# Sorting the targets of a sparse graph attention in two groups by node, with the edge marks made by ScalarE

## What is computed

```python
hs = layer_norm(x, ln1_scale, ln1_bias)          # sources
ht = layer_norm(h_target, ln1_scale, ln1_bias)   # targets
q = (ht @ Wq + bq) / sqrt(32); k = hs @ Wk + bk; v = hs @ Wv + bv
logits = where(adj != 0, q.k per head, -1e30)
ctx = softmax(logits) @ v
ht = layer_norm(ht + ctx @ Wo + bo, ln2_scale, ln2_bias)
out = layernorm(x + ht + gelu(ht @ W1) @ W2)
```

## Time and profile before

| | |
|---|---|
| median of 3 runs | 369.51 us (369.49 to 371.01) |
| profiled execution, its own time | 366.63 us |
| its span in the trace, first to last instruction | 364.8 us |
| busy: PE, DVE, ACT, POOL | 68%, 64%, 43%, 52% |
| first gather | 132.75 us |
| start of the last gather | 289.67 us |

### The profile page before, as it was taken

How to read it: one execution, slowest core, us unless ns; L and a number is a source line. 1 busy time by engine, 2 the same in 40 slices (tenths; PEclk the granted TensorE clock), 3 DMA queues, 4 the chain that set the end, 5 groups by cost and what they waited for, 6 DMA issues and landing times. The chain is left out here.

```text
span 364.8 us, 4184 instructions
## 1 busy us (share of the span) xinstructions
PE 247.2 (68%) x1270; PEld 180.3 (49%) x1270; DVE 233.4 (64%) x648; ACT 157.8 (43%) x263; POOL 191.1 (52%) x209
## 2 busy tenths in 40 slices
PE   0339959897995020325999895879987979679900
PEld 0314413433431010215888785768876967578800
DVE  2613078989489854697798677767878679922110
ACT  0816403698766930002566652646534445223200
POOL 2699704325120037777778878887888712311210
PEclk9999967999999555555999998998999899969965
DMA  7993398999993017776765555555654610000000
GB/s 182 380 386 138 136 320 324 351 417 331 401 353 115 1 51 233 227 204 195 208 199 155 173 139 168 155 158 175 200 153 131 163 34 16 15 0 16 26 24 1
DMA packets 27972, 64.34 MB, mean 176 GB/s; under 512 B 6500, under 2 KB 14950, under 8 KB 25895
## 3 DMA queue, kind: packets, MB, share of 16 engines
q0 software_dynamic: 8368, 29.11, 27.5%
q1 hardware_dynamic: 11792, 25.44, 18.9%
q10 hardware_dynamic: 7782, 9.45, 7.3%
HBM read 53.50 MB, written 12.58 MB: 181 GB/s over the span
## 5 line engine op out<-in xcount | busy, mean ns | idle before, releaser
L610 POOL DMA_INDIRECT arena<-kv_scratch,places x79 | 92.8, 1175 | 22.7 <-issue 22.7
L797 PE MATMUL score<-h_t,w_sb 128*128 128x128 f32 x512 | 70.8, 298 | 7.3 <-ACT h_t L1073 7.2
L797 PEld LDWEIGHTS score<-h_t,w_sb 128*128 128x128 f32 x512 | 66.6, 211 | 10.6 <-ACT h_t L1073 10.6
L709 PE MATMUL bank<-arena 128*128 128x512 f32 x128 | 64.5, 643 | 10.8 <-POOLq L553 5.6
L806 PE MATMUL bank<-w_sb,gelu_t 128*128 128x256 f32 x256 | 58.3, 381 | 0.0
L806 PEld LDWEIGHTS bank<-w_sb,gelu_t 128*128 128x128 f32 x256 | 47.6, 190 | 7.9 <-ACT gelu_t L1049 1.9
L709 PEld LDWEIGHTS bank<-arena 128*128 128x128 f32 x128 | 25.6, 205 | 40.2 <-issue 39.0
L1359 DVE TENSOR_TENSOR arena<-arena,tab 128x1024 f32<-128x1024 f32 (+3 forms) x22 | 24.5, 1113 | 16.9 <-DMA arena<-kv_scratch,places 16.9
L627 POOL DMA_INDIRECT out_dram<-y_out,places x16 | 18.5, 1154 | 28.7 <-ACT y_out L1065 25.9
L606 POOL DMA_INDIRECT tab<-tab_scratch,places x16 | 15.6, 974 | 33.4 <-DVE place_value L1335 28.9
L991 ACT ACTIVATE gelu_t<-arena 128x2048 bf16<-128x2048 bf16 x16 | 30.6, 1910 | 3.8 <-issue 2.3
(11 more groups left out here) (127 smaller groups left out, 378.7 us busy)
## 6 DMA issues: line engine op xcount, KB each, us to landing
arena<-in_adj_dram SPq DMA_DIRECT2D x16, 1024.0 KB, 11.5
kv_scratch<-arena ACTq DMA_DIRECT2D x16, 256.0 KB, 5.5
tab_scratch<-arena ACTq DMA_DIRECT2D x16, 256.0 KB, 4.8
arena<-in_x_dram SPq DMA_DIRECT2D x4, 512.0 KB, 6.6
arena<-in_L_gnn_h_target_dram SPq DMA_DIRECT2D x4, 512.0 KB, 8.8
tab_scratch<-in_x_dram SPq DMA_DIRECT2D x1, 2048.0 KB, 13.8
w_sb<-in_L_gnn_W_dram SPq DMA_DIRECT2D x2, 1024.0 KB, 14.7
arena<-kv_scratch,places POOLq DMA_INDIRECT x79, 3.9
```

The costliest lines, as they stand in the source:

```text
L610: pool.indirect_dma_start(kv_ring[:, ring_at[m] + j, :], None, kv_dram[:, :], at).then_inc(gathered[m][piece], 16)
L709: mm = pe.matmul(proj_ps[n % 2], h_t[:, s, c % 2, k, i * P:(i + 1) * P], weights[:, k, :], start=(k == 0 and s == 0), stop=(k == DK - 1))
L797: mm = pe.matmul(hid_ps[2 * (n % 2) + half][:, f % 4 * P:(f % 4 + 1) * P], w1_sb[:, k, f * P:(f + 1) * P], h2_t[:, n % 2, k, :], start=(k ...
```

## The change

Targets are split by node. **Group A** holds nodes 0 to 1023 (adjacency tiles 0 to 7), of which the 128 with most sources are put off; it has 7 tiles with 2, 3, 3, 4, 5, 5, 7 slots (29). **Group B** holds the rest and those 128, in 9 tiles with 2, 3, 3, 4, 5, 5, 7, 8, 16 slots (53). Slots grow from 79 to 82, gathers from 95 to 98. Group A is sorted before the first gather; group B's quarters, its sort and its matmuls are written into steps -3 to 3 of the second stage (`PLACED` = 3). POOL waits for group A's places before step -3 and for group B's in step 3, behind that step's `rsqrt_pair`.

`find_edges` becomes one ACT pass, Relu(1 - 1e7 x), with its sum as an accumulated output, in place of DVE's pass and ACT's count. Adjacency loads 4 to 15 move from SP's queue to ACT's, each written behind a `find_edges`; from tile 10 on only two slots are left. SP takes over the saves of key and value rows, and the first four adjacency loads wait for the weights. Projection units are reordered (`UNITS`: source chunks ahead of target chunks); the last target unit is projected around group A's placement matmul.

```diff
-    SLOTS = [16, 8, 7, 6, 5, 5, 5, 4, 4, 4, 3, 3, 3, 2, 2, 2]
+    SLOTS_OF = [[7, 5, 5, 4, 3, 3, 2], [16, 8, 7, 5, 5, 4, 3, 3, 2]]
+    SKIPPED = [1, 0]
...
+    UNITS = [(0, 0), (1, 0), (0, 1), (0, 2), (1, 1), (0, 3), (1, 2), (1, 3)]
+    FIRST_UNITS = 6
...
+            def group_ready(g):
+
+                pool.wait_ge(places_ready, 3 * (g + 1))
+                pool.wait_ge(x_copied[g], 16)
+                for r in range(CT):
+                    pool.wait_ge(qh_saved[r], 16 * 2 * (g + 1))
+                if g == 0:
+                    pool.wait_ge(kv_read, TILES)
+                    for r in range(CT):
+                        pool.wait_ge(kv_saved[r], 16 * CHUNKS)
+                    pool.wait_ge(mean_saved, 16)
...
                         rsqrt_pair(pair_of_res(s + 1) if s + 1 < hi else pair_of_y(s - 1), some)
                     if lo == 0:
+                        if step == PLACED:
+                            group_ready(1)
...
+            for u in range(FIRST_UNITS):
+                project(u)
+                if u == 2:
+                    make_keys(0)
+                if u == 4:
+                    make_keys(1)
+                turn_rows(u + 2)
+            project(FIRST_UNITS)
...
+            sum_classes(0)
+            sum_ranks(0)
+            project(FIRST_UNITS + 1, range(2))
+            place(0)
+            project(FIRST_UNITS + 1, range(2, CT))
+            make_keys(2)
...
+                    if lo == 0:
+                        if s == PLACED - 5:
+                            make_keys(3)
+                        if s == PLACED - 3:
+                            sum_classes(1)
+                        if s == PLACED - 1:
+                            place(1)
...
+            def load_adj(t):
+                if t < TILES:
+                    act.wait_ge(edges_ready, (t - AR if t < EARLY + 2 else t - 2) + 1)
+                    act.dma_start(adj_tile_of(t), adj[t * P:(t + 1) * P, :]).then_inc(adj_loaded[adj_slot(t)], 16)
+
+            def find_edges(t):
+
+                act.wait_ge(adj_loaded[adj_slot(t)], 16 * adj_uses(t))
+                edges_free(act, t)
...
+                act.activation(edges_of(t), adj_tile_of(t), ACT.Relu, bias=1.0, scale=-STEEP,
+                               accum_out=tally[:, 0, t:t + 1]).then_inc(edges_ready, 1)
+                if t >= EARLY + 1:
+                    load_adj(t + 1)
...
+                    if lo == 0 and s < -1:
+                        find_edges(TILES - 4 if s == -LEAD else TILES - 2)
+                        find_edges(TILES - 3 if s == -LEAD else TILES - 1)
...
+                        if s == PLACED - 4:
+                            for n in range(QK):
+                                pick_bank(3, n)
+                            split_keys(3)
+                        if s == PLACED - 3:
+                            list_edges(3)
+                            sort_classes(1)
+                        if s == PLACED - 2:
+                            spread_totals(1)
+                        if s == PLACED - 1:
+                            sort_ranks(1)
+                        if s == PLACED:
+                            keep_places(1)
```

More of the change, by code:

```diff
@@ L47, in graph_attention @@
     COLS = sum(2 + s for s in SLOTS)
-    col_of = [sum(2 + s for s in SLOTS[:i]) for i in range(TILES)]
+    col_of = [sum(2 + s for s in SLOTS[:i]) for i in range(TILES + 1)]
+    COLS_OF = [col_of[FIRST_TILE[g + 1]] - col_of[FIRST_TILE[g]] for g in range(2)]
     QUARTERS = 4
@@ new lines, in sum_ranks, with place @@
+            def sum_ranks(g):
+                rows = NCLS * CELLS_OF[g]
+                pe.wait_ge(class_spread, g + 1)
+                pe.matmul(rank_ps[g][:, 0:rows], class_total[0:rows, :], below[0:rows, 0:rows], start=False, stop=True,
+                          skip_group_check=True).then_inc(rank_summed, 1)
+            def place(g):
+                pe.wait_ge(spread_ready, sum(len(set(SLOTS_OF[o])) for o in range(g + 1)))
+                for c in range(CELLS_OF[g]):
+                    if c % QT == 0:
+                        pe.wait_ge(lo_ready, g * CELLS_OF[0] // QT + c // QT + 1)
+                    mm = pe.matmul(place_ps[g][:, 0:COLS_OF[g]], lo_hot[:, c, :], spread[:, c, 0:COLS_OF[g]], start=(c == 0),
+                                   stop=(c == CELLS_OF[g] - 1))
+                mm.then_inc(placed, 1)
@@ L1235, in _ @@
+            for u in range(3):
+                row_stats(u)
+                row_moments(u)
             dve.wait_ge(weights_loaded, 16 * N_WEIGHTS)
@@ L1323, in _ @@
-            dve.wait_ge(pick_step, listed + 10)
-            for d in sorted(set(SLOTS), reverse=True):
-                spread_class(SLOTS.index(d), SLOTS.count(d))
-            for g in range(CELLS // QT):
-                some = slice(QT * g, QT * (g + 1))
-                dve.tensor_tensor(lo_hot[:, some, :],
-                                  rank_lo[:, some].rearrange("p (c a) -> p c a", a=1).to_broadcast([P, QT, P]),
-                                  numbers[:, :].rearrange("p (a n) -> p a n", a=1).to_broadcast([P, QT, P]),
-                                  ALU.is_equal).then_inc(lo_ready, 1)
```

782 lines of the change are left out of this document (451 added, 331 removed).

## The result

| | before | after |
|---|---|---|
| median | 369.99 us (369.49 to 371.01, 4 runs) | 407.45 us (403.52 to 409.75, 4 runs) |
| profiled execution, its own time | 366.63 us | 409.51 us |
| its span | 364.8 us | 407.8 us |
| first gather | 132.75 us | 115.78 us |
| root of step 3 | 207.22 us | 217.43 us |

The ratio is 1.097, 95% interval 1.087 to 1.108: slower by a tenth. The forecast was 390 us, with a range of 366 to 403.

A forecast was written before the change was run, and what follows sets the result against it. The prediction took POOL's gathers to set the pace from 133 to 291 us, at 1.46 us a row. It summed 104 + 100.4 + 181.2 to a 385.6 us span, plus 4.7 to about 390 us, range 366 to 403.

The forecast's parts named there:

- Sign and mechanism: Whole kernel: first gather 29 us earlier, 26 lost until step 3, 24 more for 17 more rows left; slower 0.81.
- From the first gather to the root of step 3: Second stage's start, with group B's quarters and sort between steps on DVE: 100.4 us, against 74.5 before.
- The value of 7 us: Time taken for each 1 MB adjacency load ahead of ACT's last passes, three of them one after another.
- The estimate of 6.8 us: Same 1 MB load, with half of the DMA rate left beside the gathers; the sum would be unchanged.
- The 4.4 us for 1 MB alone: Same load by a fixed 2.0 us plus bytes/436e3; the sum would be 8 us less.
- Until the first gather: First stage, by PE's units, ACT's passes and group A's sort: 104 us (97 to 113), against 132.75 before.
- the first stage does not come forward: Rival, first stage: ACT bounds it or its issues block; first gather 115 to 120; with slow loads, chance 0.15.
- From the root of step 3 to the end: Rest of the second stage and tail: 181.2 us against 157.6, from 17 more rows, one more save, 2.6 less tail.
- the edge that the prediction named as a sign of being wrong: POOL's gathers of group B: the prediction is wrong if rows come at less than 1.4 us each.
- The forecast said that DVE keeps up: Behind step 3's root: DVE needs 8 us of edges and 2.6 of statistics a step, against POOL's 13 us.
- The correction from span to median: Added to the span: 1.8 us to the execution's own time and 2.9 more to the median, 4.7 in all.
- The rival of POOL's pace: Rival, second stage: group B fits DVE's idle time, step 3's root 74.5 us after first gather; 364 us, chance 0.14.

The follow-up runs named there:

- one_pass: Kernel before, with DVE's compare and ACT's count replaced by one ACT pass for the edge marks, nothing else of the change: 372.43 us, 0.8% slower.
- again: The changed kernel once more, unedited, to measure its own spread: 404.01 us, ratio 1.095 to the kernel before.
- h_first: Changed kernel, with the last h_target quarter's load ahead of three late weight loads and the third key/value save on SP's queue: 398.93 us, ratio 1.078.
- place_first: Changed kernel, with PE's `place(0)` ahead of both halves of the last projection instead of between them: 405.93 us, ratio 1.101.
- busy: Kernel before, with 80 repeats of a small DVE operation added right behind the places: 385.42 us, ratio 1.037.
- roots_first: Changed kernel, h_target load and late passes forward, group B sorted in one piece, ten tab slots, each step's rows behind its root: 366.73 us, ratio 0.997.
- load_ahead: Changed kernel, adjacency loads from tile 10 issued ahead of the previous tile's pass but behind the wait for that tile: 405.70 us, ratio 1.098.
- load_first: Changed kernel, adjacency loads from tile 10 issued ahead of ACT's wait for the tile before, passes where they were: 399.92 us, ratio 1.081.
- passes_early: Changed kernel, adjacency loads from tile 10 ahead of the wait for the tile before, passes 12 to 15 moved earlier: 394.56 us, ratio 1.067.

## Why the prediction was half right

**Sign and mechanism: right.** The split was forecast to win at the first gather and to lose more behind it, POOL having nothing to gather while DVE sorts group B between steps.

**From the first gather to the root of step 3: right, term by term.** Forecast 100.4 us, measured 101.65. Pass 12 was put at 16.3 us behind the first gather and began at 17.7; three loads at 7 us each measured 7.1, 7.1 and 7.3; the root of step -1 was put at 52.3 and began at 52.8. The other marks, forecast in brackets: root of step 0 at 64.1 (64.5), of step 1 at 71.7 (73.6), of step 2 at 87.1 (88.5), the places at 95.6 (93). One term did not fit the others: POOL was to wait ahead of the root of step -1 from 35 to 48 us, although that root was put at 52.3; it waited from 31.7 to 52.8, and its rows of group A ended at 75 us, not at 60. Neither moved the sum, since DVE set it.

The value of 7 us carried this stretch, and it was a choice between the least, 5.0, and the median, 11.5, of the earlier trace rows, which no row settled: with either of these the sum would have been 94 or 114 us. That it hit was in part luck. The estimate of 6.8 us from the Trainium skill's page "DMA: Bandwidth & Descriptors", section "Queues, rings and completion order", was nearly as near. Its reason, that the gathers take half of the rate, is not borne out: the third load took 7.3 us from 147.65 us on, and POOL's last gather before it had been issued at 146.47 us. The 4.4 us for 1 MB alone come from that page's section "Anatomy of one DMA", which states the formula for DMAs issued by GpSimd, while these loads are ACT's and SP's; the shortest adjacency load of any run took 4.7 us (one_pass).

**Until the first gather: the step that failed.** Forecast 104 (97 to 113), measured 115.78, 11.8 us of the 22.2 us by which the span came out longer. The sum took the order of units on PE and ACT's passes into account, but put SP's queue at nothing: the last h_target chunk stands there behind `save_kv(2)`. That wait on SP is worth 7.9 us against the profiled execution and 9.7 against again (h_first); without it the first gather is at 107.85, within the forecast's bounds, and the time at 398.93, within the range. The other 3.9 us were not taken apart. The mean row, which the prediction called hidden behind the sort, was so only because the half projection in front of `place(0)` was longer: with that away it was the last (place_first). The rival "the first stage does not come forward" gave 115 to 120 us and 402 to 406 us; the first gather came out there and the time 1.5 us above, but its mechanism, ACT's issues and passes as the bound, is not what the runs showed.

**From the root of step 3 to the end: mis-sized.** Forecast 181.2, measured 190.4. Of these 9.2 us, 4.7 lie before the last gather. The groups of POOL there, by form, first of before, then of after:

```profile
L610 POOL DMA_INDIRECT arena<-kv_scratch,places x41 | 50.2, 1224 | 11.5 <-issue 11.5
L627 POOL DMA_INDIRECT out_dram<-y_out,places x7 | 8.6, 1231 | 2.1 <-issue 2.1
L620 POOL TENSOR_TENSOR rstd_late<-var_late,minus_half 128x2 f32<-128x2 f32 x8 | 5.9, 733 | 0.2
L606 POOL DMA_INDIRECT tab<-tab_scratch,places x4 | 3.8, 955 | 1.2 <-issue 1.2
```

```profile
L710 POOL DMA_INDIRECT arena<-kv_scratch,places x53 | 58.0, 1095 | 15.3 <-issue 15.0 <-DVE var_late L1676 0.3
L706 POOL DMA_INDIRECT tab<-tab_scratch,places x9 | 10.9, 1216 | 2.5 <-issue 2.5
L727 POOL DMA_INDIRECT out_dram<-y_out,places x8 | 9.6, 1200 | 3.8 <-ACT y_out L1248 1.9 <-issue 1.5 <-DVE var_late L1676 0.3
L720 POOL TENSOR_TENSOR rstd_late<-var_late,minus_half 128x2 f32<-128x2 f32 x9 | 9.6, 1066 | 14.1 <-DVE var_late L1676 14.0
```

A row cost (58.0 + 15.3 + 10.9 + 2.5)/62 = 1.40 us, less than the 1.46 forecast and at the edge that the prediction named as a sign of being wrong, so that the rows added 20.0 us for 24.8. Three other terms ran over. The sum had left out that one more root comes with one more save, and the roots are 1066 ns each for 733: 3.7 us for nothing. The saves added 2.7 us for 1.45. And POOL waits for DVE: of the 14.0 us, 9.55 stand ahead of step 3's root, the other 4.5 are new. The forecast said that DVE keeps up.

The other 4.5 us are the tail, 77.0 for 72.5. One step was gone from it, as forecast (five roots behind the last gather for six), but this saved nothing: the last context came 31.4 us behind the last gather for 31.2, and the end 45.7 us behind that for 44.0. At the statistics of one step DVE now waits 2.74 us for PE (355.05 us), for 0.34 before (313.77 us).

**The correction from span to median** (4.7 us) did not hold: after, the median lay 0.35 us below the profiled span. This was luck: the miss of the span was 22.2 us, that of the time 17.5.

**The rival of POOL's pace** needed group B to fit into DVE's idle time. It did not in any order that was run. The extra 26.6 us of DVE's work come at a time when POOL's root, and with it POOL, waits for DVE, and of 26.4 us added there to the kernel before, 14.8 reached the end (busy). In roots_first, the best order I found, the 25.4 us won at the first gather are spent as 21.9 us between it and the end: 23.9 us ahead of the root of step -1, where DVE is busy 24.2 us longer, less 1.9 us behind it. So the three rows more and the steps behind that root are not the loss. Whether an order exists that puts group B's work into DVE's remaining 12 us of idle time there, no run shows.

## What to carry to other kernels

A stage that starts early on half of its data wins only as far as the other half's preparation fits into what the engines leave idle just behind the new start; count the busy time there, not its share of the span (64% for DVE here). Where a queue issues both gathers and small results that a chain waits for, put the result first. When loads and saves share one queue in order, list everything that stands ahead of each load, and what each of those waits for, before pricing the stage.

## What the runs showed of the hardware that was not expected

Cost of a wait ahead of an issue: a 1 MB load issued behind ACT's wait for the tile before (load_ahead) left 0.4 us ahead of the pass and its pass came no earlier than with the issue behind the pass, while the same line ahead of the wait (load_first) brought the passes to 4.6 to 6.9 us apart. A load with another in flight took 11 to 12 us to its pass (passes_early) for 7.1 to 7.3 alone. GpSimd's `pow` on 2 columns took 733 ns in the mean before (8 of them, 207.2 to 289.8 us) and 1066 ns after (9, 217.4 to 330.9 us), at the same shape; the runs don't show why.
